# Attention kernel of four layers: group 1's head outputs moved by DMA beside group 0's before the division and the projection

## The reference

```
q, k, v = (split_heads(q), split_heads(k), split_heads(v))
attn = jax.nn.softmax(jnp.einsum('bhqd,bhkd->bhqk', q, k), axis=-1)
o = jnp.einsum('bhqk,bhkd->bhqd', attn, v)
o = o.transpose(0, 2, 1, 3).reshape(B, H * W, Cc)
o = o @ wp.T + bp
return o.transpose(0, 2, 1).reshape(B, Cc, H, W) + x
```

## Time and profile before

| | |
|---|---|
| median of 3 runs | 6464.93 us (6464.25 to 6472.68) |
| profiled execution, its own time | 6474.8 us |
| its span, first to last instruction | 6473.0 us |
| TensorE busy | 6135.6 us (95%), mean granted clock 0.972 |
| VectorE, ScalarE, GpSimd busy | 3980.8, 4142.4, 3434.3 us |

### The profile page before, as it was taken

One profiled execution on the slowest core, in us unless ns is written; L12 is line 12 of the kernel. 1 busy time (PEld: TensorE's weight loads), 2 busy tenths in 40 slices (PEclk: granted clock), 3 DMA queues, 4 the chain that ended last, 5 costly groups with the idle time before them and its releaser, 6 DMA issues.

```text
span 6473.0 us, 80369 instructions
## 1 busy us (share of the span) xinstructions
PE 6135.6 (95%) x29648; PEld 2935.1 (45%) x29648; DVE 3980.8 (61%) x4659; ACT 4142.4 (64%) x5828; POOL 3434.3 (53%) x2738
## 2 busy tenths in 40 slices
PE   5789999999999999999999999999999999999986
PEld 2334444444444444444444444444444444444333
DVE  1566666666666666666666666666666666666541
ACT  2356666666666666666666666666666666666552
POOL 4236555555555555655555555555565555556333
PEclk7799999999999999999999999999999999999987
DMA  1011011011101101101101110110110110111000
GB/s 34 4 24 25 14 28 28 18 28 24 27 15 28 26 20 28 24 15 27 28 18 28 24 28 14 28 27 18 28 24 16 26 28 18 28 25 28 11 14 7
DMA packets 95783, 145.66 MB, mean 23 GB/s; under 512 B 60320, under 2 KB 62496, under 8 KB 95264
## 3 DMA queue, kind: packets, MB, share of 16 engines
q1 hardware_dynamic: 95392, 140.53, 9.9%
HBM read 18.07 MB, written 16.78 MB: 5 GB/s over the span
## 4 chain that ended last, share of the span: by engine, by line
PE 83%; DVE 9%; ACT 4%; issue 2%; POOL 1%; DMA 0%; SPq 0%; POOLq 0%; ACTq 0%; DVEq 0%
PE p_chain L1172 18%; PE p_sc L1172 16%; PE p_max L1172 15%; PE p_acc L1172 13%; PE p_full L1172 12%; PE p_head L1172 10%; DVE mx_half L1017 3%; DVE f2mx L1012 2%; ACT p L881 1%; ACT hx L765 1%; ACT fp L850 0%; ACT exact L785 0%; DVE f_num L1050 0%; DVE x L1081 0%; DVE f0mx L1012 0%
## 5 line engine op out<-in xcount | busy, mean ns | idle before, releaser
L1017 DVE TENSOR_REDUCE mx_half<-p_max 128x2 f32<-128x1024 f32 x2048 | 2508.5, 1225 | 1436.4 <-PE p_max L1172 1431.1
L881 ACT ACTIVATE p<-p_head 128x1024 f32<-128x1024 f32 x2048 | 2101.5, 1026 | 1131.4 <-PE p_head L1172 996.3
L708 POOL TENSOR_TENSOR fp_lo<-fp,fp_hi 128x512 fp32r<-128x512 f32 x1024 | 1315.1, 1284 | 1780.2 <-ACT fp L850 1773.7
L1172 PE MATMUL p_acc<-p,v 128*17 128x512 f32 x8192 | 1089.4, 611 | 0.1
L1172 PE MATMUL p_max<-ks,qs 63*128 63x512 f32 x4096 | 988.4, 479 | 69.8 <-DVE mx_half L1017 61.0
L1172 PE MATMUL p_head<-qs,ks 64*128 64x512 f32 x4096 | 971.4, 470 | 38.7 <-ACT p L881 37.9
L729 POOL TENSOR_TENSOR fsum<-fsum,fp 128x512 f32<-128x512 f32 x768 | 987.3, 1286 | 4.6
L840 ACT ACTIVATE fp_hi<-p_sc 128x512 fp32r<-128x512 f32 x1024 | 611.6, 597 | 583.9 <-PE p_sc L1172 429.6
L1172 PEld LDWEIGHTS p_head<-qs,ks 64*128 64x128 f32 x4096 | 388.4, 186 | 776.5 <-ACT p L881 428.4
L1172 PEld LDWEIGHTS p_max<-ks,qs 63*128 63x128 f32 x4096 | 387.1, 186 | 698.1 <-DVE mx_half L1017 462.1
L850 ACT ACTIVATE fp<-p_sc 128x512 f32<-128x512 f32 x1024 | 611.7, 597 | 1.2 <-POOL fsum L725 1.1
(11 more groups left out here) (184 smaller groups left out, 8431.9 us busy)
## 6 DMA issues: line engine op xcount, KB each, us to landing
qs<-cq_hi SPq DMA_DIRECT2D x128, 256.0 KB, 4.6
ks<-ck_hi SPq DMA_DIRECT2D x128, 256.0 KB, 4.6
x_in<-x_dram SPq DMA_DIRECT2D x32, 512.0 KB, 3.4
qs<-cq_lo SPq DMA_DIRECT2D x64, 256.0 KB, 4.4
ks<-ck_lo SPq DMA_DIRECT2D x64, 256.0 KB, 5.2
out_dram<-x SPq DMA_DIRECT2D x32, 512.0 KB, 2.8
zrow<-rz SPq DMA_DIRECT2D x128, 16.0 KB
cw<-packed_dram SPq DMA_DIRECT2D x1, 1178.0 KB, 5.4
```

Source lines behind the costliest of these rows:

```text
L708: pool.tensor_tensor(fp_lo[u % 2][:, :], fp[u % 2][:, :], f32(fp_hi[u % 2][:, :]), ALU.subtract).then_inc(f.plo, 1)
L881: act.activation(p1[slot][:, 2 * pr:2 * pr + 2, :], P_HEAD[:, :].rearrange("p (e n) -> p e n", e=2), ACT.Exp, scale=float(DH) ** -0.5).the ...
L1017: dve.reduce_max(mx_half[:, pr, :, t, kh], P_MAX[:, :].rearrange("p (e n) -> p e n", e=2), AX.X)\
L1172: return pe.matmul(dst, lhsT, rhs, start=start, stop=stop)
```

## The change

The tile `o1[0]` gets the heads of group 1 in the 16 rows that were zero: head j of group 1 goes from rows 32j to 32j+15 of `o1[1]` to rows 32j+16 to 32j+31 of `o1[0]`. Eight DMA transfers of 16 rows by 512 columns do it, four for each half (`o_move`), after the last round and after group 0's sums have been read. The division for group 0 in mid-period falls away; one spread with a matrix of 16 rows, one division and one projection matmul with the merged weights `wp1m` serve both groups, once per half. `wp1m` is filled at the start by eight small transfers, for which all engines wait. The matmul that builds `spread_r` at the start is now two. Where a step waited for group 0's division only to know that `p_chain` was free, it waits for `m_neg` now. All tables of places are new numbers.

```diff
-SPREAD = 32 + 2 * G1
+SPREAD = 4 * G1
...
-PLACE = dict(h0=4.2, hp0=3.139, h1=111.45, hp1=2.884, exp=-0.09, pv=4.06, out=2.68, ma=7.77,
...
+PLACE = dict(h0=4.23, hp0=3.138, h1=111.42, hp1=2.884, exp=-0.06, pv=4.07, out=5.02, ma=7.88,
...
+             spread01=128.54, divide01=131.95, omv0=204.58, omv1=204.68, proj0=12.75,
...
-    o_rb = 4
-    o_n = 4
+    o_mv = 4 * 16
+    o_rb = 2
+    o_n = 2
...
-                for h in range(2):
-                    at(PLACE[f'spread{g}{h}'], "o_spread", k, g, h); at(PLACE[f'divide{g}{h}'], "o_divide", k, g, h)
             for h in range(2):
+                at(PLACE[f'omv{h}'], "o_move", 0, h); at(PLACE[f'spread1{h}'], "o_spread", -1, h); at(PLACE[f'divide1{h}'], "o_divide", -1, h)
...
+            for h in range(HEADS):
+                row = 32 * (h % G1) + DH * (h // G1)
+                sp.dma_start(wp1m[row:row + DH, :],
+                             packed[DH * h:DH * (h + 1), COL["wp1"]:COL["wp1"] + C])\
+                    .then_inc(s_const, 16)
...
+            def o_move(b, h):
+
+                sp.wait_ge(sem.o_ev, b.at(PER.o_ev, 3 + h))
+                sp.wait_ge(sem.o_r, b.at(PER.o_r, 1))
+                for j in range(G1):
+                    sp.dma_start(o1[0][32 * j + DH:32 * (j + 1), half(h)],
+                                 o1[1][32 * j:32 * j + DH, half(h)]).then_inc(sem.o_mv[h], 16)
+
             def o_return(b, g):
                 sp.wait_ge(sem.o_r, b.at(PER.o_r, g + 1))
 
-                after(sp, (sem.o_rb, b.shift(-1), PER.o_rb, 2 * g + 2))
+                after(sp, (sem.o_rb, b.shift(-1), PER.o_rb, 2))
                 for part in range(2):
-                    row = 32 * g + G1 * part
+                    row = 2 * G1 * g + G1 * part
                     sp.dma_start(f32(zrow[row:row + G1, :]), f32(rz2[:, g, part, :]))\
                         .then_inc(sem.o_row, 16)
...
-            def o_divide(b, g, h):
-                dve.wait_ge(sem.o_rb, b.at(PER.o_rb, 2 * g + h + 1))
-                dve.tensor_tensor(o1[g][:, half(h)], o1[g][:, half(h)], P_CHAIN[:, :], ALU.mult)\
+            def o_divide(b, h):
+                dve.wait_ge(sem.o_mv[h], b.at(PER.o_mv, PER.o_mv))
+                dve.wait_ge(sem.o_rb, b.at(PER.o_rb, h + 1))
+                dve.tensor_tensor(o1[0][:, half(h)], o1[0][:, half(h)], P_CHAIN[:, :], ALU.mult)\
                    .then_inc(sem.o_n, 1)
 
...
-                          (sem.o_n, b.shift(-1), PER.o_n, 2),
+                          (sem.m_neg, b.shift(-1), PER.m_neg, 2),
...
-            def o_spread(b, g, h):
+            def o_spread(b, h):
                 if h == 0:
-                    pe.wait_ge(sem.o_row, b.at(PER.o_row, (g + 1) * 32))
-                    if g == 0:
-                        pe.wait_ge(sem.m_neg, b.at(PER.m_neg, 2))
-                    else:
-                        after(pe, (sem.m_neg, b.shift(1), PER.m_neg, 1),
-                              (sem.t_ev, b.shift(-1), PER.t_ev, 2), (sem.o_n, b, PER.o_n, 2))
-                else:
-                    pe.wait_ge(sem.o_n, b.at(PER.o_n, 2 * g + 1))
-                r = slice(32 * g, 32 * g + 2 * G1)
-                mm(P_CHAIN[:, :], spread_r[r, :], zrow[r, half(h)]).then_inc(sem.o_rb, 1)
+                    pe.wait_ge(sem.o_row, b.at(PER.o_row, PER.o_row))
+                    after(pe, (sem.m_neg, b.shift(1), PER.m_neg, 1),
+                          (sem.t_ev, b.shift(-1), PER.t_ev, 2), (sem.m_neg, b, PER.m_neg, 2))
+                else:
+                    pe.wait_ge(sem.o_n, b.at(PER.o_n, 1))
+                mm(P_CHAIN[:, :], spread_r[:, :], zrow[0:SPREAD, half(h)]).then_inc(sem.o_rb, 1)
 
             def o_project(b, h):
                 if h == 0:
-                    pe.wait_ge(sem.o_n, b.at(PER.o_n, 4))
+                    pe.wait_ge(sem.o_n, b.at(PER.o_n, 2))
                 else:
                     pe.wait_ge(sem.o_x2, b.at(PER.o_x2, 1))
-                for g in range(2):
-                    last = mm(P_CHAIN[:, :], mat(("wp1a", "wp1b")[g]), o1[g][:, half(h)],
-                              start=g == 0, stop=g == 1)
-                last.then_inc(sem.o_pj, 1)
+                mm(P_CHAIN[:, :], wp1m[:, :], o1[0][:, half(h)]).then_inc(sem.o_pj, 1)
 
...
-                    after(pe, (sem.o_n, b.shift(1), PER.o_n, 2),
+                    after(pe, (sem.m_neg, b.shift(1), PER.m_neg, 2),
...
-            pe.wait_ge(s_const, 32)
-            pe.wait_ge(s_ones, 12)
+            pe.wait_ge(s_const, 16 * (2 + HEADS))
+            pe.wait_ge(s_ones, 13)
```

More of the change, by code:

```diff
@@ new lines @@
+HEAD_MOVE = [1.54, -0.41, -0.29, -1.46, -3.17, -4.24, -3.27, -1.72, -0.98, -2.68, -4.35, -5.25,
[5 rows of a table added]
+MAX_MOVE = [-0.2, -0.69, -1.66, -0.62, -2.17, -3.42, -4.24, -5.03, -0.45, 1.01, -1.31, -1.03,
[4 rows of a table added]
+HEAD_SUM_MOVE = [1.12, 2.39, 8.27, 1.37, 3.52, 3.66, -0.24, -3.35, 1.15, 1.15, 1.74, -0.76,
+                 -1.16, 3.2, 12.3, 3.06, 0.81, -1.75, 1.63, -0.09, 0.04, 4.72, 3.81, -3.04, 0.29,
+                 -2.43, 2.35, -2.14, 4.29, 2.62, 2.09, -2.05]
+FULL_MAX_MOVE = {0: [3.89, 2.66, 6.5, 4.9, 4.45, 4.78, 5.46, 6.99],
+                 2: [-3.3, -3.74, -2.98, -0.94, -1.94, 1.78, 4.54, 5.27]}
@@ new lines @@
+FULL_MOVE = {0: [-10.74, -3.48, -2.49, -3.7, -2.17, -2.84, -3.79, -3.07, -0.74, 0.07, 1.39,
+                 -0.59, -2.56, -1.44, -4.57, 1.22],
+             2: [-4.89, -4.84, 2.42, 0.94, 3.89, 1.93, -1.0, -2.9, 0.41, -2.71, -1.15, -5.21,
+                 -6.72, -4.79, -5.83, -5.52]}
+FULL_SUM_MOVE = {0: [6.85, 2.11, -2.46, 3.28, 0.76, 0.16, 6.45, 1.05, -0.52, 1.77, -1.7, 3.03,
+                     0.45, -3.3, -2.54, -1.03],
+                 2: [1.66, 7.45, 4.24, 3.76, -1.21, -3.24, 2.58, 1.43, 1.33, -0.38, -4.64, -0.67,
+                     0.36, -0.78, 1.17, -1.18]}
@@ L309, in __init__ @@
         self.o_row = new("o_row")
+        self.o_mv = [new(f"o_mv{h}") for h in range(2)]
         self.o_rb = new("o_rb")
@@ L347, in heads_kernel @@
         const_bias = sb("const_bias", [C, 2])
-        lane_of = sb("lane_of", [C, G1])
-        zpad = sb("zpad", [C, SPREAD])
+        lane_of = sb("lane_of", [C, 2 * G1])
+        zpad = sb("zpad", [C, 2, SPREAD])
+        wp1m = sb("wp1m", [C, C])
         spread_r = sb("spread_r", [SPREAD, C], F32R)
@@ L408, in heads_kernel @@
         t_sq = sb("t_sq", [C, T, 2, D3])
-        lanes, turn = (t_sq[:, 4 * k:4 * k + 4, :, :].rearrange("p t a d -> p (t a d)")
-                       for k in range(2))
+        turn = t_sq[:, 0:4, :, :].rearrange("p t a d -> p (t a d)")
+        lanes = [f_num[:, C * g:C * (g + 1)] for g in range(2)]
         t_ns = sb("t_ns", [C, T * 2])
@@ L628, in _ @@
             play(sp, dict(load=load, stack=stack, m_row=m_row, o_gather=o_gather,
-                          o_return=o_return, f_gather=f_gather, f_return=f_return, store=store))
+                          o_move=o_move, o_return=o_return, f_gather=f_gather, f_return=f_return, store=store))
             sp.wait_ge(sem.stored, 16 * images)
@@ L1135, in t_scale @@
                                   .broadcast_to([C, T, D3 + 1]), ALU.mult).then_inc(sem.t_qs, 1)
-            dve.wait_ge(s_const, 32)
-            dve.wait_ge(s_ones, 12)
-            dve.reduce_sum(lane_of[:, :], mat("ident").rearrange("p (j c) -> p j c", c=32), AX.X)\
+            dve.wait_ge(s_const, 16 * (2 + HEADS))
+            dve.wait_ge(s_ones, 13)
+            dve.reduce_sum(lane_of[:, :], mat("ident").rearrange("p (j c) -> p j c", c=DH), AX.X)\
                .then_inc(s_lanes, 1)
-            for start in (0, 32):
-                dve.tensor_copy(zpad[:, start:start + 2 * G1].rearrange("p (a j) -> p a j", a=2),
+            for g in range(2):
+                dve.tensor_copy(zpad[:, g, 2 * G1 * g:2 * G1 * (g + 1)]
+                                .rearrange("p (a j) -> p a j", a=2),
                                 col("zsel", G1).rearrange("p (a j) -> p a j", a=1)
@@ L1146, in _ @@
             dve.wait_ge(s_lanes, 3)
-            dve.tensor_copy(lanes.rearrange("p (j a) -> p j a", j=G1), lane_of[:, :].rearrange("p (j a) -> p j a", a=1)
-                            .broadcast_to([C, G1, 32])).then_inc(s_lanes, 1)
+            for g in range(2):
+                dve.tensor_copy(lanes[g].rearrange("p (j a d) -> p j a d", j=G1, a=2)[:, :, g, :],
+                                lane_of[:, :].rearrange("p (j a) -> p j a", a=2)[:, :, 1:2]
+                                .broadcast_to([C, G1, DH])).then_inc(s_lanes, 1)
             for dst, name in ((wq1, "wq1"), (wk1, "wk1"), (turn, "ident")):
@@ L1434, in _ @@
             mm(P_CHAIN[:, 0:W3], col("bv2").broadcast_to([C, C]), col("w3", W3)).then_inc(s_fold, 1)
-            pe.wait_ge(s_lanes, 16)
-            mm(P_SC[0:SPREAD, 0:C], zpad[:, :],
-               lanes).then_inc(s_fold, 1)
+            pe.wait_ge(s_lanes, 17)
+            mm(P_SC[0:SPREAD, 0:C], zpad[:, 0, :], lanes[0], stop=False)
```

(1 more changed line is left out.)

51 lines of the change are left out of this document (32 added, 19 removed), and 18 rows, old and new, of tables (HEAD_MOVE, MAX_MOVE).

## The result

The changed kernel takes 6492.17 us (median of 7 runs, 6489.85 to 6500.45) against 6469.2 us of the kernel before (7 runs on the same chip, 6464.25 to 6474.71). The ratio is 1.0038 with a 95% interval of 1.0026 to 1.005: **0.4% slower**, where the prediction said 6424 and faster. The time lies just inside the range given (6370 to 6495), on the side of the rivals.

A forecast was written before the change was run, and what follows sets the result against it. TensorE, busy 98%, was taken as the bound. Per image -2.46 + 1.4 - 0.5 = -1.56 us; over 31 seams -48, with +7 for the ends -41, so 6424 us from a median of 6464.93; range 6370 to 6495.

The forecast's parts named there:

- The new order elsewhere: All stages' matmuls interleave anew: one p_sc wait goes, other chains tighten; -0.5 us an image, bounds -1 and +3.
- rival (3): New order brings its own waits: 3 us an image more gives 6517; with (4), 0.16 within 0.2%, 0.11 beyond.
- TensorE's work, -2.46: Per image on TensorE, two of four spreads go (0.84 us) and the projections shrink (1.62 us).
- The wait at the seam, 1.4: Between images, TensorE's first head scores wait 1.4 us for the maxima row behind eight moves; bounds none and 5.5.
- Start, +5: At the run's start, ten constant transfers instead of two delay TensorE's first matmul by 5 us, bounds 2 and 7.
- An issue doesn't end before the third one ahead of it has landed: Reading of SyncE's queue at the seam, used to time the eight moves and the constant loads at the start.
- Tail, +2: In the last image, eight moves of 0.6 us lie between gather and return, 2.91 us apart before: +2 us.
- The count of 31: The per-image change of -1.56 us is counted over 31 seams, giving -48 us.
- (1): Moves at the seam are hidden: -2.96 us an image, -85 in all, 6380 us; chance 0.15.
- (4): TensorE isn't the bound, removed work becomes idle: 6464 or a little over; with (3), 0.16 within 0.2%, 0.11 beyond.
- the 0.4 that the prediction worked out beside: By the Trainium skill's dispatch figure, about 50 ns, eight moves hold SyncE 0.4 us and the 1.4 wait vanishes.
- (2): Moves cost the crowded queue's 1.27 us each: wait 5.5 us, +2.54 an image, 6551 us; chance 0.08.

The follow-up runs named there:

- Experiment 3: Kernel before, its computation unchanged and without moves, given only the changed kernel's tables of places: 6545.0 us, ratio 1.0119 to the kernel before.
- experiment 2: Merged computation with the tables of the kernel before, first half's four moves issued ahead of the stack transfers: 6407.4 us, ratio 0.9903 to the kernel before.
- experiment 4: Changed kernel with the first half's four moves issued ahead of the stack transfers: 6476.89 us, ratio 1.0012 to the kernel before.
- experiment 1: Merged computation with the tables of the kernel before, all eight moves between group 1's gather and m_row: 6461.84 us, ratio 0.9988 to the kernel before.
- 8: Changed kernel with first half's moves early, value groups 11, 12 ahead of scores 13, 14, and layer 0's start reordered: 6421.47 us, ratio 0.9925 to kernel before.
- 10: Kernel before, in its own order, with the eight moves added at the seam and their data unused: 6614.02 us, ratio 1.0229.

## Why the prediction was wrong

**The step that failed** is "The new order elsewhere ... I take -0.5 for all of it, with bounds of -1 and +3". Experiment 3 has it alone: +2.95 us an image, at the very upper bound. With it the sum closes: -2.0 for the merge (experiment 2), +2.95 for the order, +0.15 for the moves (changed kernel against experiment 4, 192.27 - 192.12) are +1.1, and +1.15 was measured. (The merge enters from the old order; in the new order it is worth -1.95, so the two effects add up nearly without touching each other.) The reading of the order rows was one-sided: it looked for the wait that a wider spacing would take away, and found it, and did not walk the other waiting chains through the new rows. Both places could have been found there. At the seam `fp` has two buffers, and value group 11 slid behind scores 13; at the start of layer 0 two `p_head` pairs stand one `p_max` pair apart. The text had even named this case as rival (3) and argued "the steps kept nearly the same neighbours", which was untrue at exactly those two places. The other half of the order's cost, the 1.6 us of busy time in experiment 3, belongs to no wait; the prediction has no term for it, and its cause stays open.

**TensorE's work, -2.46.** Experiments 1 to 4 give -2.0 (191.12 against 189.1 in the old order, 194.07 against 192.12 in the new). The single step was nearly right: the projection goes from 3132.23 to 3133.39 in the changed kernel, 1.16 for the 1.05 assumed. The images at full clock shown under experiments 3 and 8 give, between the kernel before and experiment 2, 2.3 us less busy time and 0.1 more idle time (2.2 and 0.2 in the mean of such images). So some 0.25 of the missing 0.46 is work that didn't go and 0.2 is new idle time.

**The wait at the seam, 1.4.** Right in size where it stands alone: 1.2 in experiment 1, 1.3 in 10, and the eight issues take 5.83 us for the 5.8 to 6.4 assumed. What it cost *in the changed kernel* was 0.15, since TensorE came late for another reason; that was the lower bound ("none, if TensorE comes to the scores later for another reason"), and the other reason was the failed step. Alone it costs more than its length, by the clock: 1.46 between experiments 1 and 2.

**Start, +5.** Wrong. The eight loads of `wp1m` take 0.48 us of issue each and TensorE starts at 8.01 for 7.22: +0.8. "An issue doesn't end before the third one ahead of it has landed" fits the rows of the stack (256 KB each) and not these small loads: an issue ends 1.9 us after the third one ahead of it began, and the soonest of them lands after 2.9. **Tail, +2**: gather and returns are 5.83 apart for 2.91, +2.9.

**The count of 31.** With +1.15 for 31 images the loss would be 36 us; the spans differ by 15. The first projection of the run comes at 441.3 for 447.3, and from the row of the last image but one (6007.96 after, 5981.29 before) to the end the changed kernel is some 12 us faster. That the places with waits have no work there would fit, but was not tested. A pace holds for the images in which all layers are under way.

**Rivals.** (1) and (4) fell: the moves are not hidden in the old order (they hold SyncE for 5.83 us, not for the 0.4 that the prediction worked out beside), and a microsecond taken from TensorE was worth 0.8. (2) fell: 0.73 us a move, not 1.27. (3) is what happened, with 2.95 + 0.5 = 3.4 us more than assumed. By the rival's own scale that is +65 us; it came to +23 because the wait for the moves lay inside the order's (1.25 us an image) and the first and last images were quicker.

## What to carry to other kernels

When a change comes with a new table of places, time the new table on the old computation and the old table on the new computation first: here the computation was worth -1.0% (with its moves out of the way) and the table +1.2%, and only their sum was visible. Predict an order by walking every buffer that has one or two copies through the new rows (who frees it, how many steps ahead of its next user), not by looking at the neighbours of the changed step; and don't take the waits found so for the whole price, they were half of it here. And put transfers that nobody is waiting for ahead of the crowded stretch of a queue: four of eight moves issued some 40 us earlier were worth 54 us.
